# A decoder's first stage (RWKV time mixing) rewritten: one maximum scan, a ratio form, split weights

## What is computed

```python
x_prev = jnp.concatenate([jnp.zeros_like(x[:, :1, :]), x[:, :-1, :]], axis=1)
xk = x_prev + (x - x_prev) * tmk          # the same with tmv, tmr
k = jnp.einsum('bth,oh->bto', xk, Wk) + bk   # v, r alike
# scan over t, state aa = bb = 0, pp = -1e30, decay = -exp(time_decay), bonus = time_first
ww = bonus + kt;  p = jnp.maximum(pp, ww)
e1 = jnp.exp(pp - p);  e2 = jnp.exp(ww - p)
out = (e1 * aa + e2 * vt) / (e1 * bb + e2)
ww2 = pp + decay;  p2 = jnp.maximum(ww2, kt)
e1 = jnp.exp(ww2 - p2);  e2 = jnp.exp(kt - p2)
aa, bb, pp = e1 * aa + e2 * vt, e1 * bb + e2, p2
...
out = jnp.einsum('bth,oh->bto', jax.nn.sigmoid(r) * wkv, Wo) + bo
```

## Time and profile before

| | us |
|---|---|
| median of three runs | 1591.7 |
| the profiled execution | 1597.39 |
| its span, first to last instruction | 1595.6 |
| PE, DVE, ACT, POOL busy over the span | 1339.1, 1099.5, 810.9, 629.7 |
| first stage: first scan of DVE | 26.90 |
| first stage: starts of the scans of groups 1, 2, 3 | 61.45, 98.63, 135.79 |
| next stage: first instruction of DVE | 177.37 |

### The profile page before, as it was taken

The page is one execution under the profiler, slowest core; times in us unless marked ns, Lnnn a source line. Parts: engine busy times, 40 slices in busy tenths (PEclk is TensorE's granted clock), DMA queues, the critical chain, the costliest instruction groups (busy, mean ns, idle before and its releaser), DMA issues. The chain is left out here.

```text
span 1595.6 us, 26439 instructions
## 1 busy us (share of the span) xinstructions
PE 1339.1 (84%) x7985; PEld 1027.9 (64%) x8032; DVE 1099.5 (69%) x2086; ACT 810.9 (51%) x1811; POOL 629.7 (39%) x693
## 2 busy tenths in 40 slices
PE   6775278888699999984898998998998788987998
PEld 3332155555588888873677776777776465656887
DVE  5999588889456767568777777777776466653443
ACT  2222078888454343435565665665665255652332
POOL 3220466556561000006666566656665333220000
PEclk9988589999799999996999999999999799998999
DMA  9000133331000000002000000000000000000000
GB/s 367 41 0 0 40 99 87 79 79 40 1 1 1 1 0 0 1 1 96 1 1 1 0 0 0 0 0 0 0 0 1 5 3 3 2 1 1 14 13 27
DMA packets 30303, 40.24 MB, mean 25 GB/s; under 512 B 4320, under 2 KB 25824, under 8 KB 28704
## 3 DMA queue, kind: packets, MB, share of 16 engines
q1 hardware_dynamic: 30240, 39.45, 7.9%
HBM read 28.96 MB, written 2.10 MB: 19 GB/s over the span
## 5 line engine op out<-in xcount | busy, mean ns | idle before, releaser
L1704 ACT ACTIVATE wi_weights<-wi_psum,wi_bias,wi_scale 128x128 f32<-128x128 f32 x256 | 113.9, 454 | 113.0 <-DVE wi_bias L1814 113.0
L1479 POOL TENSOR_TENSOR wi_straight<-wi_straight,wi_crossed 128x512 f32<-128x512 f32 x80 | 110.0, 1374 | 5.8 <-DVE wi_crossed L1800 5.7
L846 DVE TENSOR_REDUCE gq_top<-gq_psum 128x4 f32<-128x512 f32 x128 | 86.8, 678 | 32.0 <-PE gq_psum L733 31.2
L1467 POOL TENSOR_TENSOR wi_scratch<-wi_sums,wi_eps 128x4 f32<-128x4 f32 x80 | 35.9, 449 | 159.7 <-DVE wi_sums L1783 158.3
L1805 DVE TENSOR_REDUCE wi_top<-wi_psum 128x4 f32<-128x512 f32 x64 | 44.0, 688 | 74.7 <-PE wi_psum L1594 74.7
L800 ACT ACTIVATE gq_weights<-gq_weights 128x512 f32<-128x512 f32 x128 | 81.1, 634 | 25.2 <-DVE gq_weights L854 23.9
L1018 POOL TENSOR_TENSOR ex_scratch<-ex_squares,ex_eps 128x4 f32<-128x4 f32 x12 | 2.4, 201 | 231.0 <-ACT ex_junk L1129 231.0
L740 PE MATMUL gq_psum<-const,gq_weights 128*128 128x128 f32 x512 | 79.3, 278 | 14.9 <-ACT gq_weights_t L806 14.9
L1215 DVE TENSOR_TENSOR ex_gated<-ex_gated,ex_psum 128x512 f32<-128x512 f32 x64 | 43.9, 687 | 65.2 <-PE ex_psum L1070 53.9
L1142 ACT ACTIVATE ex_hidden_high<-ex_gated 128x512 fp32r<-128x512 f32 x64 | 40.4, 632 | 93.8 <-DVE ex_gated L1215 93.8
L854 DVE TENSOR_TENSOR gq_weights<-gq_psum,gq_top 128x512 f32<-128x512 f32 x128 | 87.2, 681 | 0.0
(11 more groups left out here) (339 smaller groups left out, 4086.0 us busy)
## 6 DMA issues: line engine op xcount, KB each, us to landing
gq_keys<-in_ctx_keys_dram SPq DMA_DIRECT2D x16, 512.0 KB, 3.8
gq_keys_diagonal<-gq_key_parts SPq DMA_DIRECT2D x64, 128.0 KB, 3.8
x<-in_x_dram SPq DMA_DIRECT2D x4, 512.0 KB, 9.3
gate<-in_gate_dram SPq DMA_DIRECT2D x2, 1024.0 KB, 5.5
up<-in_up_dram SPq DMA_DIRECT2D x2, 1024.0 KB, 7.5
down<-in_down_dram SPq DMA_DIRECT2D x2, 1024.0 KB, 9.3
wq<-in_wq_dram SPq DMA_DIRECT2D x1, 2048.0 KB, 19.6
wo<-in_wo_dram SPq DMA_DIRECT2D x1, 2048.0 KB, 25.5
```

Of the source, the lines that this page charges most:

```text
L846: dve.tensor_reduce(top[:, u % 4, :], rows(u), AX.X, ALU.max).then_inc(topped, 1)
L1479: added_up = pool.tensor_tensor(straight[:, at], straight[:, at], crossed[:, at], ALU.add)
L1704: act.activation(weights[:, g % 2, j, :], ps[:, SC + g % 2, j * P:j * P + P], ACT.Exp, bias=bias[:, g % 2, j:j + 1], scale=scale[:, g, j:j ...
```

## The change

Only `load`, `rwkv`, the SP program of `gqa` and the semaphores in `decoder` change.

- **Projections.** The token shift goes into the weights: W times tm on the token now and W times (1 - tm) on the token before. These weights and h are split into high and low fp32r parts (ACT rounds, DVE takes the difference), and high x high, low x high and high x low are summed: 72 matmuls of 512 columns per group. POOL's `diff` is gone.
- **Scan.** The maximum is scanned per chunk; z = k - pp(before). ACT forms both scan weights from z with a Relu and an exponential. The output is (aa + rho v) / (bb + rho) with rho = exp(min(z + first, 40)), so that the second maximum, its two exponents and two products go. POOL forms e2 v.
- **Order.** ACT normalises. DVE's reciprocal and product for group g - 1 stand in group g, ahead of that group's sums, and its additions behind them. PE puts bo into PSUM with a matmul of one row of ones, and output(g - 1) stands between two projections of group g + 1.
- **Loads.** x's first part and the k weights go ahead of the constants; wq, wk, wv and wo are loaded in the first two steps of `gqa`, since their tiles hold the split weights before. Each wait for a load has a semaphore of its own, and SP clears the first stage's semaphores behind `gqa`'s last transfer.

```diff
-    sp.dma_start(net.const[:], dram["const"]).then_inc(net.in_small, 16)
-    sp.dma_start(net.rows[:], dram["rows"]).then_inc(net.in_small, 16)
...
+    load_x(0)
+    sp.dma_start(net.rwkv_w[:, 0], dram["rwkv_w"][:, 0]).then_inc(net.in_rwkv[0], 16)
+    sp.dma_start(net.const[:], dram["const"]).then_inc(net.in_const, 16)
...
+            def one(g, first, last):
+                pool.wait_ge(weight, 3 * g + 1)
+                pool.wait_ge(taken, 3 * KC * g + 2 * KC)
+                pool.tensor_tensor(tokens(e2v), tokens(e2), tokens(v), ALU.mult).then_inc(e2v_ready, 1)
...
+            def project(g, m):
+                first = isinstance(g, int) and g == 0
+                for oc in range(KC):
+                    need(pe, taken, 3 * KC * (g - 1) + KC * m + oc + 1)
+                    bank = ps[:, 2 + 2 * m + oc, :].rearrange("p (j t) -> p j t", t=P)
+                    pe.wait_ge(padded, KC * (g + 1))
+                    for step, (w, h) in enumerate(((w_high, h_high), (w_low, h_high), (w_high, h_low))):
...
+                        if step == 2:
+                            pe.wait_ge(lowered, KC * (g + 1))
+                        for now in range(2):
+                            for c in range(KC):
+                                mm = pe.matmul(bank, w[:, m, now, c, oc * P:oc * P + P], tokens(h, 1 - now, c),
...
+            def bias(g, last):
+                if not last:
+                    pe.wait_ge(lowered, KC * (g + 3))
+                need(pe, added, GB * g)
+                bo = net.rows[0:1, ROWS["L0_attn_bo"]].unsqueeze(1).broadcast_to([1, 2, D])
...
+            def one(g, first, last):
                 if not last:
                     turn(g + 1)
+                    project(g + 1, 0)
+                if first:
+                    pe.wait_ge(net.in_rwkv[3], 16)
+                    pe.wait_ge(net.in_rows, 16)
+                else:
+                    bias(g - 1, last)
                 if not last:
+                    project(g + 1, 1)
+                if not first:
+                    output(g - 1)
+                if not last:
+                    project(g + 1, 2)
...
+            def weigh(g):
+                for c in range(KC):
+                    act.wait_ge(z_ready, KC * g + c + 1)
+                    own.did(act.activation(tokens(e2, 0, c), by_row(z, c), ACT.Relu,
+                                           bias=neg_decay[:, c:c + 1], scale=-1.0))
+                for c in range(KC):
+                    own.did(act.activation(tokens(e1, 0, c), by_row(z, c), ACT.Relu, bias=exp_decay[:, c:c + 1]))
+                own.wait(own.n - KC)
+                act.activation(tokens(e2), tokens(e2), ACT.Exp, scale=-1.0).then_inc(weight, 1)
+                own.wait()
+                act.activation(tokens(e1), tokens(e1), ACT.Exp, scale=-1.0).then_inc(weight, 1)
+                act.wait_ge(capped, KC * (g + 1))
+                act.activation(rho[:], rho[:], ACT.Exp).then_inc(weight, 1)
...
             def one(g, first, last):
                 if not last:
+                    normalise(g + 1)
+                    pad_h(g + 1)
+                weigh(g)
+                if not last:
+                    for m in range(3):
+                        take(g + 1, m)
...
+            def lower(g):
+                for c in range(KC):
+                    dve.wait_ge(padded, KC * g + c + 1)
+                    need(dve, projected, 3 * KC * g)
+                    dve.tensor_tensor(tokens(h_low, 0, c), ps[:, c, :].rearrange("p (j t) -> p j t", t=P),
+                                      tokens(h_high, 0, c).bitcast(F32), ALU.subtract).then_inc(lowered, 1)
...
+            def divide(g):
+                dve.wait_ge(er_read, g + 1)
+                for i in range(2):
+                    own.did(dve.reciprocal(by_pair(den, i), by_pair(den, i)))
+                    own.wait()
+                    dve.tensor_tensor(by_pair(rw, i), by_pair(num, i), by_pair(den, i),
+                                      ALU.mult).then_inc(rw_ready, 1)
...
+            def accumulate(g):
+                dve.wait_ge(weight, 3 * g + 2)
+                own.did(dve.tensor_tensor_scan(state["bb"][:, 1:], e1[:], e2[:], 0.0, ALU.mult, ALU.add))
+                dve.wait_ge(e2v_ready, g + 1)
+                own.did(dve.tensor_tensor_scan(state["aa"][:, 1:], e1[:], e2v[:], 0.0, ALU.mult, ALU.add))
...
             def one(g, first, last):
-                scan(g, None if last else g + 1, first)
+                scan(g)
+                if not last:
+                    lower(g + 1)
+                if not first:
+                    divide(g - 1)
+                accumulate(g)
+                if not first:
+                    add(g - 1)
...
+                if isinstance(t, int) and t < 2:
+                    load_attn1(nc, net, (("wq", "wk"), ("wv", "wo"))[t])
```

More of the change, by code:

```diff
@@ L34 @@
 FAR = -1e30
+CAP = 40.0
 ROW = P + 1
@@ L395, in _, with scan @@
             own = Own(dve, own_dve)
-            def link(instruction):
-                own.wait(own.did(instruction))
-            def normalise(g):
-                need(dve, turned, g)
-                for j in range(GB):
-                    b = GB * g + j
-                    h = dve.tensor_scalar(h_tok[:, j, :], net.x[:, b, :], net.mean_var[:, b, 0:1],
-                                          net.rstd[:, bass.ds(b, 1)], ALU.subtract, ALU.mult)
-                h.then_inc(normed, 1)
-            def scan(g, more, first):
-                dve.wait_ge(taken, 3 * KC * g + KC)
-                link(dve.tensor_tensor_scan(state["pp"][:, 1:], flat(decay), flat(k), FAR, ALU.add, ALU.max))
-                need(dve, rw_ready, g)
+            def scan(g):
@@ L421, in scan @@
-                if more is not None:
-                    normalise(more)
+                    own.wait(own.n - KC + 1 + c)
+                    dve.tensor_tensor(by_row(z, c), tokens(k, 0, c), before("pp", c),
+                                      ALU.subtract).then_inc(z_ready, 1)
                 for c in range(KC):
-                    own.did(dve.scalar_tensor_tensor(by_row(peak[:], c), tokens(k, 0, c), col(FIRST, c),
-                                                     before("pp", c), ALU.add, ALU.max))
@@ L427, in scan @@
-                own.wait()
-                for c in range(KC):
-                    dve.tensor_tensor(tokens(f1, 0, c), before("pp", c), by_row(peak[:], c),
-                                      ALU.subtract).then_inc(exponent, 1)
-                for c in range(KC):
-                    dve.scalar_tensor_tensor(tokens(f2, 0, c), tokens(k, 0, c), col(FIRST, c),
-                                             by_row(peak[:], c), ALU.add, ALU.subtract).then_inc(exponent, 1)
-                if not first:
-                    add(g - 1)
```

291 lines of the change are left out of this document (150 added, 141 removed).

## The result

The changed kernel takes 1577.3 us (median of 5 runs, 1575.5 to 1579.9) against 1596.2 for the kernel before (5 runs, 1590.4 to 1597.7, on the same chip): ratio 0.9888, 95% interval 0.9872 to 0.9905. So it is faster, by 19.0 us. Forecast were 1563 us and 28.4 us less, with 1554 to 1574 as the range: the time lies outside it. The profiled execution took 1575.5, its span is 1573.5; before, 1597.4 and 1595.6. The span is 22.1 us shorter, and 21.0 of that lie in the first stage: its last instruction on DVE ends at 156.0 us, where 148.7 was forecast, and the next stage begins at 156.3 instead of 177.4. From there to the end it takes 1417.2 us against 1418.2 before, and DVE's first reduction of scores in the next stage comes 20.9 us after that stage's start in both. So the moved loads cost nothing that can be seen.

What follows compares the result with a forecast made beforehand. DVE bounds the first stage until the PE and ACT loop is as long; the stage was to end at 148.7 instead of 177.1, 28.4 us less, so profiled 1569.0, less 5.7 gives 1563 us, range 1554 to 1574.

Steps and rivals of the forecast that it cites:

- the ring of PE and ACT: First stage, per group: project, take, normalise, transpose, pad, project again; 26.7 us, or 28.7 with the clock's fall.
- its single fall of the clock: PE's clock falls in each of three gaps between groups' projections; the next ten matmuls run slower, +2.0 us per round.
- the conversion from the profiled execution to the median: Whole kernel: the median of the runs was put 5.7 us below the profiled execution of 1569.0, giving 1563.
- DVE's groups: First stage: DVE's own instructions were summed to 26.4 us a group, against 37.2 before.
- The wait before L477: Sign of being right: DVE waits for h_high in group 2 before forming h's low part, with periods of 26 to 29 us.
- The start: First stage's beginning: x's statistics at 4.7 us, first projection at 13.3; DVE ends group 0 at 51.4, gaining only 2 us.
- POOL beside DVE: POOL's product beside DVE's reciprocal costs 0 from group 1 on, at most 5.7 us in all; 1 us charged in group 0.
- rival 2: More is lost: two of reciprocal contention, later x, slower hand-offs or delayed keys; +7 us, 1570; chance 0.20.
- Rival 1: PE's clock holds in the gaps; the stage ends at 144.7, 32.4 us saved, 1559; chance 0.24.
- Rival 3: A little more is gained by earlier x, shorter hand-offs and the clock kept: 1553; chance 0.04.
- Rival 4: PE's projections: fp32r matmuls with moving rows 129 words apart take 0.43 us each; +16.5, 1608; chance 0.04.
- Rival 5: ACT's serial order idles DVE in every group, 7 us more in each of three; 1584 or above; chance 0.03.

Runs made afterwards that it cites:

- experiment 7: Changed kernel with early normalising, bias matmul over all 128 partitions, and both reciprocals ahead of both half products in every group but the last: 1555.6 us, ratio 0.9758.
- experiment 2: Changed kernel with the bias matmul reading all 128 partitions instead of one: 1573.3 us, ratio 0.987.
- experiment 5: Changed kernel with twelve useless matmuls filling PE's gap before each turn of transposes: 1573.1 us, ratio 0.9869.
- experiment 3: Changed kernel with the product e2*v moved from POOL to DVE, behind the first sum scan: 1575.4 us, ratio 0.9887.
- experiment 1: Changed kernel with ACT normalising group g+2 right after taking the keys of group g+1: 1560.5 us, ratio 0.9788.
- experiment 8: Kernel of experiment 7 with transposes between the halves of the last projection and, in group 0, e2 made before r is taken: 1559.2 us, ratio 0.9789.

## Why the prediction was wrong

The direction and the place were right, and so was the mechanism in the main: DVE's work shrinks until the ring of PE and ACT is as long, and the clock falls in its gap. What failed are sizes, and a second fall that no term stood for. Two steps carry the miss: the ring, with its single fall of the clock, which helped to put the stage's end 7.3 us late, and the conversion from the profiled execution to the median, 7.5 us. Either alone would have left the time inside the stated range (at about 1570 in both cases).

**DVE's groups.** 26.7 us of work, 26.4 forecast; but that is luck in part, for two errors cancel. 1.6 of the 26.7 are the half product that POOL held back, which the forecast put at nothing. Without it, in experiment 7, a group lasts 25.0: the forecast added up durations, and each instruction starts about 0.1 us before the one ahead of it ends (the two scans are counted as 4.6, and from 74.25 to 78.67 are 4.4). The wait before L477, which the forecast named as a sign, is 4.1 us for the lowering of group 3, where 2.5 were counted (86.0 to 88.5).

**The ring, the first step that failed.** "The projections are 72 fp32r matmuls" and "the new bias matmuls four halves of 0.43 = 1.7", in all 28.7 us with one fall of the clock, were 31.1. Piece by piece, from project(2) to project(3): projection 0 with its fall 7.3 (7.5 forecast), bias and projection 1 9.2 (7.2), output 3.3 (3.5), projection 2 6.0 (5.5), gap 5.4 (4.9). (The sum itself went on with a gap of 4.7, from 83.8 to 88.5, and so with a ring of 28.5.) So the largest term is one that was missing: a second fall of the clock in each ring, behind the bias matmul (experiment 2). I had priced that matmul by its duration and taken for granted that PE at work holds its clock. In the gap normalising four tiles takes 2.07 us where I had taken 1.5 from the 407 ns of L1121. That row is a plain rounding; L388, with its scale and its shift read from tiles, takes 588 ns, and four of them start 0.5 us apart. The first fall was right in kind. That projection 0 was met as well (7.3 and 7.5) is again two errors: experiment 5 prices the fall at 1.5 us (7.32 to 5.85), where I had 2.0, and the six steps at full clock at 5.85, where I had 5.5.

**The start.** The first projection began at 14.46 instead of 13.3: statistics at 5.47 instead of 4.7, and the same 0.5 us of normalising. project(0) ended at 33.9 instead of 31.9, and the gap behind it was 6.0 instead of 4.9, with 0.6 of normalising again and 0.9 of transposes at the lower clock in it. Why x's statistics began 0.8 later than counted no run shows. The weights of group 0 came 2.9 us late (44.1 instead of 41.2), and with them group 1's scan (54.85 instead of 51.4).

**POOL beside DVE.** The reciprocal is free of it, as taken. But the product that stands between the two reciprocals has two SBUF inputs and is not, and I had priced only the reciprocal. 1.6 us in groups 1 and 2, which the ring hid, and 2.1 in group 3, which shows. In group 0 it was 1.35 where I charged 1. In experiment 3 the last group gets 0.8 us shorter, after paying for the product on DVE. POOL's product takes 2.4 us there, where 1.7 to 1.9 was taken.

**The sum.** project(1) begins 3.1 us late (39.9 against 36.8), project(2) 3.9 (63.9 against 60.0), project(3) 6.5 (95.0 against 88.5); group 3 ends 8.3 late (143.3 against 135.0), the stage 7.3, since the tail is 12.7 instead of 13.7. So the start gave 3.1, the first ring 0.8, the second 2.6, the last group 1.8, and the tail took 1.0 back. That is rival 2's size, 7 us, and partly its make (x later, longer hand-offs), but not its main causes. Rival 1 is out: the clock did fall. Rival 3 is out. Rival 4 is out: L319 starts 0.235 us apart at full clock. Rival 5 is nearest in kind: ACT's serial order does idle DVE in groups 1 and 2, by 4.3 and 4.1 us and not 7. Moving one ACT step (experiment 1) gives back 14 us, twice the miss.

**The time itself, the second step that failed.** I set the median 5.7 us below the profiled execution, as before. That was no offset but scatter: of eleven runs of the kernel before in the last comparison four lay at 1591.0 to 1591.8 and six at 1595.2 to 1597.3, and the three runs shown had two of the lower kind. The new kernel's median lies 1.8 us above its profiled execution. So 7.5 us of the 14.3 between 1563 and 1577.3 come from here and 7.3 from the stage; the later stages give 1.0 back, and 0.5 are rounding and a profiled execution that lies 2.0 us above its span and not 1.8.

## What to carry to other kernels

When a change takes work off the engine that binds, write down the next ring of engines instruction by instruction, and look in it for steps that need not stand there: an ACT step that depends on nothing recent (the normalising) held a gap open by 3.2 us a group and, with the clock that the pause lost, cost 14 us of the stage. Count a GpSimd product against every two-input DVE instruction that can meet it, not only the long one, and put it beside one-input work. Add up distances between starts and not durations. A forecast of a time should rest on ratios or on several runs of before, not on the distance between one execution and the median of three.

## What was not expected of the hardware

PE's clock fell while PE was busy without a break: behind four halves of a matmul over one partition (1*128, 1x512; 1.98 us) the granted clock went from 1.00 to 0.50 within 3 us, in 8 of 12 cases, and never behind the same matmul over 128 partitions (1.88 us, 8 cases). That is a count over few cases and not a mechanism; no run shows why it falls there. One partition saves no time either: 1.98 us against 1.88. The Trainium skill (TensorE: Matmul & The Clock Gate, section "Why this matters for your kernels") says that a single matmul over 32 partitions takes the same time as one over 128. No run here has 32, but the trace agrees in that the one with fewer is not shorter. The pause in the ring is firmer. With ACT's normalising in it (2.7 to 3.0 us of standing still before the transposes and 1.3 behind) the next projection began at half clock in all 15 rounds of five traces; without (1.2 to 1.3 us behind the transposes alone) in none of 9 rounds of three traces. Why 4 of 12 biases kept the clock stays open. So does what lies between: behind 1.84 us of standing still it fell in group 1 of one kernel (experiment 8) and not in its groups 2 and 3, and behind 2.74 us the transposes of group 1 ran at 1.97 us in one execution of the new kernel and at 1.09 in another.
